# Linear attention in a fused transformer block: each head's kv and output as a product of its own, two heads on halves of TensorE's array

## The reference

```python
h = concatenate([tok(x), txt], axis=1)            # (4, 1024, 256)
y = layernorm(h)
q = elu(split_heads(y @ Wq)) + 1                  # 16 heads, 64 channels
k = elu(split_heads(y @ Wk)) + 1
v = split_heads(y @ Wv)
g = sigmoid(split_heads(y @ Wg + bg))
kv = einsum('bhnd,bhne->bhde', k, v)              # one 64 x 64 matrix a head
k_sum = k.sum(axis=-2)
z = 1.0 / clip(einsum('bhnd,bhd->bhn', q, k_sum), 1e-6)
out = einsum('bhnd,bhde->bhne', q * 64 ** -0.5, kv) * z[..., None] * g
h = h + merge_heads(out) @ Wo
# then two layers of local attention and gated FFN on layernorm(h)
```

## Time and profile before

| | us |
|---|---|
| median of 3 runs (1953.76 to 1954.8) | 1953.86 |
| the profiled execution | 1955.45 |
| its span, from the first to the last instruction | 1953.7 |
| PE busy | 1863.4 (95%) |
| PE weight loads busy | 1624.6 (83%) |
| DVE busy | 1522.5 (78%) |
| ACT busy | 1094.7 (56%) |

### The profile page before, as it was taken

How to read it: one execution, slowest core, us unless ns; L and a number is a source line. 1 busy time by engine, 2 the same in 40 slices (tenths; PEclk the granted TensorE clock), 3 DMA queues, 4 the chain that set the end, 5 groups by cost and what they waited for, 6 DMA issues and landing times. The chain is left out here.

```text
span 1953.7 us, 40490 instructions
## 1 busy us (share of the span) xinstructions
PE 1863.4 (95%) x13340; PEld 1624.6 (83%) x13340; DVE 1522.5 (78%) x4717; ACT 1094.7 (56%) x2551; POOL 431.3 (22%) x319
## 2 busy tenths in 40 slices
PE   8899999999999799999998799979999999989998
PEld 8789889899898578888887688867888888878887
DVE  6888878878687688888887577768888888867777
ACT  4433433433432578888887334427787778853333
POOL 0000000000000335444543000013544454411010
PEclk9999999999999899999999899989999999999999
DMA  9100000000010100000000200010000000000002
GB/s 342 43 1 1 1 1 1 1 1 1 11 57 1 50 7 5 5 5 5 5 4 11 85 12 11 11 44 4 6 4 5 5 5 4 5 22 12 11 11 91
DMA packets 44980, 44.46 MB, mean 23 GB/s; under 512 B 8359, under 2 KB 39387, under 8 KB 44894
## 3 DMA queue, kind: packets, MB, share of 16 engines
q1 hardware_dynamic: 44894, 43.33, 6.7%
HBM read 34.93 MB, written 8.39 MB: 22 GB/s over the span
## 5 line engine op out<-in xcount | busy, mean ns | idle before, releaser
L1117 ACT ACTIVATE l_probs<-l_probs,l_negmax 128x256 f32<-128x256 f32 x512 | 253.2, 496 | 64.8 <-DVE l_negmax L1224 64.8
L1075 POOL TENSOR_TENSOR l_t<-l_t,l_rnorm 128x512 f32<-128x512 f32 x128 | 131.0, 1044 | 301.7 <-DVE l_rnorm L1241 301.7
L117 PE MATMUL ps<-local_w_hi,l_xT 128*128 128x512 f32 x384 | 167.5, 436 | 25.2 <-DVE l_xT L1184 16.1
L1070 POOL TENSOR_TENSOR l_t<-l_t,l_t 128x1024 f32<-128x1024 f32 x64 | 152.6, 2384 | 146.0 <-DVE l_t L1270 146.0
L1123 ACT ACTIVATE l_probsT<-ps 128x512 f32<-128x512 f32 x256 | 138.4, 594 | 40.3 <-PE ps L1375 40.2
L118 PE MATMUL ps<-local_w_lo,l_xT 128*128 128x512 f32 x384 | 155.5, 405 | 0.0
L119 PE MATMUL ps<-local_w_hi,l_xT 128*128 128x512 f32 x384 | 154.5, 402 | 0.0
L117 PE MATMUL ps<-m_hnT_hi,ffn_w_hi 128*128 128x512 f32 (+1 forms) x352 | 143.5, 408 | 10.4 <-DVE m_u L1642 6.1
L486 ACT ACTIVATE attn_exp<-ps 128x512 f32<-128x512 f32 x128 | 76.5, 600 | 133.1 <-PE ps L119 133.1
L1375 PE MATMUL ps<-ident,l_probs 128*128 128x128 f32 x1024 | 135.2, 276 | 6.2 <-ACT l_probsT L1123 6.2
L118 PE MATMUL ps<-m_hnT_lo,ffn_w_hi 128*128 128x512 f32 (+1 forms) x352 | 140.3, 399 | 0.0
(11 more groups left out here) (252 smaller groups left out, 5823.5 us busy)
## 6 DMA issues: line engine op xcount, KB each, us to landing
tok_x<-x SPq DMA_DIRECT2D x16, 512.0 KB, 8.2
m_shifted<-shifted SPq DMA_DIRECT2D x20, 256.0 KB, 2.7
shifted<-x SPq DMA_DIRECT2D x64, 64.0 KB, 1.5
out<-x SPq DMA_DIRECT2D x8, 512.0 KB, 4.5
ffn_w_raw<-ffn_w SPq DMA_DIRECT2D x6, 640.0 KB
local_w_raw<-ffn_wqkv SPq DMA_DIRECT2D x4, 768.0 KB, 5.0
tok_base<-attn_base SPq DMA_DIRECT2D x4, 512.0 KB, 8.7
h<-txt SPq DMA_DIRECT2D x4, 512.0 KB, 8.4
```

What stands on the lines that cost most here:

```text
L117: nc.tensor.matmul(out, wh, mh, start=start, stop=False, skip_group_check=True)
L1070: nc.gpsimd.tensor_tensor(t1[:], t1[:], t2[:], ALU.add).then_inc(s.summed.sem, 1)
L1075: nc.gpsimd.tensor_tensor(v, v, rn[:, a * LH:(a + 1) * LH].unsqueeze(2).to_broadcast([P, LH, DH]), ALU.mult).then_inc(s.rotated.sem, 1)
L1117: last = nc.scalar.activation(v, v, ACT.Exp, bias=nb[:, h:h + 1], scale=-1.0, accum_out=rsum[:, h:h + 1])
```

## The change

`kv_products` and `outputs` make one product for each head in place of one for each pair. In `kv_products` a head's 64 columns of G are the weights and its 65 columns of `attn_wv` the moving side; the two heads of a pair write partitions 0 to 63 and 64 to 127 of the same columns, and so use the two halves of the array's columns. In `outputs` a head's 64 partitions of `attn_qT` and `attn_kv` are used, in the two halves of the array's rows; the even heads write bank 4 and the odd heads bank 5. `attn_kv` then has 65 columns a pair and no zeros, and `take_kv` is two copies. A tile has two groups of 4 pairs, and each of them uses both banks: the next group waits until `gated` has emptied them, for which `attn_o` is counted twice a group. `kv_products` waits for the pieces of G in two steps. Wv is loaded into rows of 64 elements in place of 128.

```diff
-    VC = P + 1
-    OC = P + 2
-    GROUPS = ((0, 3), (3, 6), (6, 8))
-    KV_BANKS = (4, 5, 3)
+    OC = DH + 1
+    PG = PAIRS // 2
...
             def gated(b, n, *groups):
                 for g in groups:
-                    m0, m1 = GROUPS[g]
-                    w = m1 - m0
-                    dve.wait_ge(*s.attn_o_full.after(OB * b + 3 * n + g + 1))
-                    out = ps[:, 4 + (3 * n + g) % 2, 0:w * OC].rearrange("p (m c) -> p m c", c=OC)
...
+                    done = OB * b + 4 * n + 2 * g
+                    dve.wait_ge(*s.attn_o_full.after(FB * b + 2 * n + g + 1))
+                    out = ps[:, 4:6, 0:PG * OC].rearrange("p e (m c) -> p m e c", c=OC)
...
+                    chain(nc.vector.tensor_scalar(heads(zd[:]), out[:, :, :, DH:OC], 1e-6, 2.0 * DH ** 0.5, ALU.max, ALU.mult))
+                    chain(nc.vector.reciprocal(z[:], zd[:]))
+                    nc.vector.tensor_tensor(o1[:, g].rearrange("p (m e d) -> p m e d", e=2, d=DH), out[:, :, :, 0:DH],
+                                            heads(z[:]).to_broadcast([P, PG, 2, DH]), ALU.mult).then_inc(s.attn_o.sem, 1)
+                    dve.wait_ge(*s.attn_o.after(done + 1))
                     if g == 0:
                         dve.wait_ge(*s.attn_b_done.after(GB * b + 2 * n + 2))
...
+                    nc.vector.scalar_tensor_tensor(og[:, n % 2, cols], th[:, n % 2, cols], 1.0, o1[:, g],
+                                                   ALU.add, ALU.mult).then_inc(s.attn_o.sem, 1)
...
             def take_kv(b):
 
                 dve.wait_ge(*s.attn_kv_mm.after(b + 1))
-                dve.wait_ge(*s.attn_set.after(1))
-                for g, (m0, m1) in enumerate(GROUPS):
-                    acc = ps[:, KV_BANKS[g], 0:(m1 - m0) * VC].rearrange("p (m c) -> p m c", c=VC)
-                    for e in range(2):
-                        r = slice(e * DH, (e + 1) * DH)
-                        nc.vector.tensor_copy(kv[r, m0:m1, e * DH:(e + 1) * DH], acc[r, :, e * DH:(e + 1) * DH])
-                        done = nc.vector.tensor_copy(kv[r, m0:m1, P + e:P + e + 1], acc[r, :, P:VC])
+                for g in range(2):
+                    done = nc.vector.tensor_copy(kv[:, g * PG:(g + 1) * PG, :],
+                                                 ps[:, 4 + g, 0:PG * OC].rearrange("p (m c) -> p m c", c=OC))
...
             def kv_products(b):
-                pe.wait_ge(*s.attn_gt.after(4 * b + 4))
-                for g, (m0, m1) in enumerate(GROUPS):
-                    for m in range(m0, m1):
+                for g in range(2):
+                    pe.wait_ge(*s.attn_gt.after(4 * b + 2 * g + 2))
+                    for m in range(g * PG, (g + 1) * PG):
                         for c in range(KC):
-                            last = nc.tensor.matmul(ps[:, KV_BANKS[g], (m - m0) * VC:(m - m0 + 1) * VC],
-                                                    gt[:, c, m * P:(m + 1) * P], wv[:, c, m, :],
-                                                    start=(c == 0), stop=(c == KC - 1))
+                            for e in range(2):
+                                h = 2 * m + e
+                                last = nc.tensor.matmul(ps[e * DH:(e + 1) * DH, 4 + g, m % PG * OC:(m % PG + 1) * OC],
+                                                        gt[:, c, h * DH:(h + 1) * DH], wv[:, c, h, :],
+                                                        start=(c == 0), stop=(c == KC - 1))
...
-            def outputs(b, u, which, *groups):
+            def outputs(b, u, which, g):
...
-                    pe.wait_ge(*s.attn_o.room(OB * b + 3 * n + g, 2))
-                    for m in range(m0, m1):
-                        last = nc.tensor.matmul(ps[:, 4 + (3 * n + g) % 2, (m - m0) * OC:(m - m0 + 1) * OC],
-                                                qt[:, m, which * P:(which + 1) * P], kv[:, m, :],
-                                                start=True, stop=True)
-                    last.then_inc(s.attn_o_full.sem, 1)
+                pe.wait_ge(*s.attn_o.after(OB * b + 4 * n + 2 * g - 1))
+                for m in range(g * PG, (g + 1) * PG):
+                    for e in range(2):
+                        r = slice(e * DH, (e + 1) * DH)
+                        last = nc.tensor.matmul(ps[:, 4 + e, m % PG * OC:(m % PG + 1) * OC],
+                                                qt[r, m, which * P:(which + 1) * P], kv[r, m, :], start=True, stop=True)
+                last.then_inc(s.attn_o_full.sem, 1)
...
-                    outputs(b, u, 0, 0, 1)
+                    outputs(b, u, 0, 0)
                     gates(b, 2 * u + 1, (0,))
-                    outputs(b, u, 0, 2)
+                    outputs(b, u, 0, 1)
                     gates(b, 2 * u + 1, (1,))
                     outputs(b, u, 1, 0)
                     out_products(b, last, u, 1)
-                    outputs(b, u, 1, 1)
...
-                    outputs(b, u, 1, 2)
+                    outputs(b, u, 1, 1)
```

More of the change, by code:

```diff
@@ L238, in _ @@
         def _(pool):
-            nc.gpsimd.memset(K.attn_wv[:, 0, :, P:P + 1], 0.0)
+            nc.gpsimd.memset(K.attn_wv[:, 0, :, DH:DH + 1], 0.0)
         @block.scalar
@@ L419, in attention_phase @@
     (kraw,), _ = mem.place(mem.wb, mem.wa, ("attn_k", [P, 2, INNER], F32))
-    (kv, o1), _ = mem.place(K.attn_rest, mem.norm, ("attn_kv", [P, PAIRS, OC], F32), ("attn_o1", [P, 2, 384], F32))
+    (kv, o1), _ = mem.place(K.attn_rest, mem.norm, ("attn_kv", [P, PAIRS, OC], F32), ("attn_o1", [P, 2, HALF], F32))
     (qt, ex, oth, otl, z, zd), _ = mem.place(
@@ L494, in tanh_ @@
             def tanh_(b, n, halves=(0, 1)):
-                act.wait_ge(*s.attn_o.after(OB * b + 3 * (n - 1)))
+                act.wait_ge(*s.attn_o.after(OB * b + 4 * (n - 1)))
                 for half in halves:
@@ L635, in gated @@
                 for g in groups:
-                    m0, m1 = GROUPS[g]
-                    w = m1 - m0
-                    dve.wait_ge(*s.attn_o_full.after(OB * b + 3 * n + g + 1))
-                    out = ps[:, 4 + (3 * n + g) % 2, 0:w * OC].rearrange("p (m c) -> p m c", c=OC)
-                    chain(nc.vector.tensor_scalar(zd[:, 0:2 * w].rearrange("p (m e) -> p m e", e=2), out[:, :, P:OC],
-                                                  1e-6, 2.0 * DH ** 0.5, ALU.max, ALU.mult))
-                    chain(nc.vector.reciprocal(z[:, 0:2 * w], zd[:, 0:2 * w]))
@@ L647, in gated @@
+                    dve.wait_ge(*s.attn_o.after(done + 1))
                     if g == 0:
                         dve.wait_ge(*s.attn_b_done.after(GB * b + 2 * n + 2))
-                    nc.vector.scalar_tensor_tensor(og[:, n % 2, m0 * P:m1 * P], th[:, n % 2, m0 * P:m1 * P], 1.0,
-                                                   o1[:, g % 2, 0:w * P], ALU.add, ALU.mult).then_inc(s.attn_o.sem, 1)
+                    cols = slice(g * HALF, (g + 1) * HALF)
+                    nc.vector.scalar_tensor_tensor(og[:, n % 2, cols], th[:, n % 2, cols], 1.0, o1[:, g],
+                                                   ALU.add, ALU.mult).then_inc(s.attn_o.sem, 1)
@@ L713, in batch @@
                     norm.deviation(nc, chain)
-                gated(b, 0, 0, 1, 2)
+                gated(b, 0, 0, 1)
                 gated(b, 1, 0)
@@ L722, in batch @@
                     ot_lo(b, last, u, 0)
-                    gated(b, 2 * u - 1, 2)
+                    if u > 1:
+                        gated(b, 2 * u - 1, 1)
                     query_feature(b, u, 2)
@@ L843, in outputs @@
                 pe.wait_ge(*s.attn_kv.after(b + 1))
-                for g in groups:
-                    m0, m1 = GROUPS[g]
-                    pe.wait_ge(*s.attn_o.room(OB * b + 3 * n + g, 2))
-                    for m in range(m0, m1):
-                        last = nc.tensor.matmul(ps[:, 4 + (3 * n + g) % 2, (m - m0) * OC:(m - m0 + 1) * OC],
-                                                qt[:, m, which * P:(which + 1) * P], kv[:, m, :],
-                                                start=True, stop=True)
-                    last.then_inc(s.attn_o_full.sem, 1)
+                pe.wait_ge(*s.attn_o.after(OB * b + 4 * n + 2 * g - 1))
[5 more added lines that the diff above has]
+                last.then_inc(s.attn_o_full.sem, 1)
             def out_transposes(b, last, u, which):
@@ L855, in out_transposes @@
                 n = 2 * (u - 1) + which
-                pe.wait_ge(*s.attn_o.after(OB * b + 3 * n + 3))
+                pe.wait_ge(*s.attn_o.after(OB * b + 4 * n + 4))
                 for half in range(2):
@@ L903, in batch @@
                 gates(b, 0)
-                outputs(b, 0, 0, 0, 1)
+                outputs(b, 0, 0, 0)
                 gates(b, 1, (0,))
-                outputs(b, 0, 0, 2)
+                outputs(b, 0, 0, 1)
                 gates(b, 1, (1,))
@@ L910, in batch @@
                 outputs(b, 0, 1, 1)
-                outputs(b, 0, 1, 2)
                 for u in range(1, STAGES):
@@ L1958, in build @@
```

(6 more changed lines are left out.)

23 lines of the change are left out of this document (10 added, 13 removed).

## The result

The changed kernel takes 1976.5 us (median of 4 runs, 1975.03 to 1977.68) against 1954.33 (4 runs, 1953.76 to 1957.2): 1.0112 times as long, 95% interval 1.0098 to 1.0125, or about 22 us more. Forecast were 13.0 more and 1966.9, range 1955 to 1977. The profiled execution's span grew from 1953.7 to 1973.5. The first matmul of the first local attention moved from 635.5 to 657.0, so the attention and what lies ahead of it lost 21.6 us, and the later phases, which the change doesn't touch, gave 1.8 back.

The account below looks back on a forecast made before the run. PE's instruction stream was taken to bound the linear attention. Terms +20.8 (`outputs`), -8.8 (`kv_products`), +0.3 (tail) and +0.7 (Wv's load) gave +13.0 us on the median of 1953.86: 1966.9 us, range 1955 to 1977.

Parts of the forecast that it names:

- `outputs`, forecast +20.8: 64 groups of half-array products in the linear attention at 1.22 us each, 78.1 us against 57.3.
- The load at 0.107 for 128 columns: In `outputs`, loading 128 weight columns takes about 0.107 us, so a pair goes at 0.110, not 0.055.
- the switch of 0.20 on either side: Going between full-array and half-array work costs PE 0.20 us before and after each `outputs` group.
- Rival A: In `outputs` the weight load does not bind: -3.5 in place of +20.8, 1942.6 us in all; 10%.
- Rival B: The mode switch around `outputs` costs only 0.10 a side: 12.8 us less, 1954, no change; 7%.
- `kv_products`, forecast -8.8: 64-column weights, 2.17 us without a wait: 2.4 us gained in each of three batches, 1.6 in the first.
- Single buffer, forecast 0 with 0.2 us to spare: `outputs` groups now need both banks, but VectorE empties them before PE's next group: no wait, cost 0.
- Rival C: The single buffer binds, VectorE late by 0.2 to 0.5 us at 32 places: +6 to +16 us, 1973 to 1983; 15%.
- Wv's load, forecast +0.7: Wv in pieces of 256 bytes for 512 slows the token phase: nothing to 3.6 us, taken as +0.7.
- The tail, forecast +0.3: At the attention's end, the last `outputs` group's longer VectorE work lies open before the last transposes: +0.3 us.

Follow-up runs that it names:

- run 6: Changed kernel with 64 of a tile's 128 tokens as weights in `outputs`, half of the outputs left out; 1949.46 us.
- run 7: Changed kernel with `outputs` moving 33 of the 65 columns, half of each head's output left out; 1974.46 us.
- run 8: Changed kernel with each `outputs` group's four even heads first, then the four odd ones; 2008.93 us.
- run 1: Changed kernel with the last `outputs` group of a stage put back ahead of the transposes; 1969.5 us, ratio 1.0073 to the kernel before.
- run 3: Changed kernel with Wv loaded in rows of 4096 bytes into Wo's place and spread by the subtraction; 1971.6 us, ratio 1.0088 to the kernel before.
- run 2: Kernel before with the new `kv_products` and Wv layout, `outputs` by pairs of heads, eight copies in `take_kv`; 1956.37 us, ratio 1.0011.
- run 4: Changed kernel with 64 unused bytes a partition ahead of Wo; 1977.82 us.
- run 5: Kernel before with 64 unused bytes a partition ahead of Wo, nothing else changed; 1958.1 us.
- run 10: Changed kernel with the group ahead of the transposes again, Wv in 4096-byte rows, Wo 8192 bytes below its old address; 1962.0 us, ratio 1.0047 to the kernel before.
- run 11: Kernel before with Wv loaded in rows of 4096 bytes in place of 512, nothing else; 1953.9 us, ratio 1.0001.
- run 9: Kernel before with new `kv_products`, four-copy `take_kv` on two engines, 4096-byte Wv rows, Wo moved, its low part later in first batch; 1942.23 us, ratio 0.9942.

## Why the prediction was right, and where its sum was short

The direction and the mechanism were right; the size came out 9 us short, nearly all of it in terms that the sum has at zero or doesn't have. The median lies in the forecast range by 0.5 us, and two of the four executions lie above it: that the range held owes something to luck.

**`outputs`, forecast +20.8.** 64 groups at 1.24 us are 79.4 for 57.3: +22.0. The load at 0.107 for 128 columns, the switch of 0.20 on either side (0.19 and 0.20 here) and the streaming of 0.055 were each as the rows of the local attention said; runs 6 and 7 show that the weights' columns bind, and run 8 that one half alone goes at the same 0.112. Rivals A and B are out. The Trainium skill, "TensorEngine Tiling (Array Packing)", section "Theoretical Speedup", gives up to twice the rate for such a shape. No part of that came here: 16 records at half the array took 1.05 us, where 8 records of the whole array take 0.90. In `kv_products`, with 64 columns of weights, it nearly did: a pair of records takes 0.058 us where one record took 0.112.

**`kv_products`, forecast -8.8.** 2.07 us and 0.14 ahead of it for 2.17 forecast, and no wait: a gain of 2.35 a batch. In the first batch VectorE was late as said: PE's work lay 2.67 us later than before at the `queries` ahead of `kv_products` and 0.93 later at `gates`, a gain of 1.7 for 1.6. Together -8.8.

**Single buffer, forecast 0 with 0.2 us to spare.** No wait on `attn_o` in the trace: VectorE's product L641 ends at 440.98 where PE's next group starts at 441.42. Rival C is out, though it gave nearly the time that was measured, by another mechanism.

**The step that failed: the moved group.** The front part says that the group between `out_products` and the transposes is gone, and the prediction never asked what it covered. It covered `residual`, which reads the bank that the transposes fill. Price: 0.58 us in nine places, 5.2 us; putting it back gave 7 (run 1).

**Wv's load, forecast +0.7.** The attention started 1.3 us later, and rows of 4096 bytes bring 3.3 (run 3), so the load was all of it; run 6, whose clock is full up to there, starts as late as the changed kernel. The sum had 0.7 by judgement between 0 and 3.6.

**The clock, not in the sum.** The half clock behind the attention's start cost 1.7 more in the profiled execution. A fall of this kind between 62 and 71 us is in the profiles of the changed kernel and runs 2, 3, 4, 5, 7, 8, 10 and 11 and is absent before and in runs 1, 6 and 9, of which run 1 has one at 126 us. Neither the load's pieces nor the time of the start sorts them, so it is told and not explained, and it may be the execution's and not the kernel's.

**What the prediction did not price:** the shift of Wo by 64 bytes. In the kernel before a stage's two `out_products` take 2.73 and 2.82 us, a few times 2.82 and 2.82, here 2.88 and 2.87; over the attention that is 2.5 us, and run 5 has the same.

**Short waits of before that are gone, not in the sum.** Ahead of the first `outputs` of a batch PE waited 0.29 us in three batches and 0.65 in the last, in the changed kernel no longer: -1.5. The busy time of the earlier trace rows, which is of a stretch inside a batch, can't show them.

**The tail, forecast +0.3.** The last wait grew from 2.43 to about 3.0 us, some +0.6. But part of what lies behind it runs at the clock's lower level in both kernels, and in the changed one the clock came back sooner. First the kernel before, then the changed one:

```profile
624.00:628.00 4.00, 3.46 (x17) 3.09 (x16) 2.04 (x4) 0.74 (x2) 0.00 (x0) 0.50 0.00 0
628.00:632.00 4.00, 4.00 (x27) 4.00 (x27) 0.42 (x1) 0.00 (x0) 0.00 (x0) 0.71 0.00 0
```

```profile
644.00:648.00 4.00, 2.37 (x10) 2.03 (x11) 2.54 (x5) 1.19 (x2) 0.00 (x0) 0.50 0.00 0
648.00:652.00 4.00, 4.00 (x26) 4.00 (x26) 0.93 (x3) 0.00 (x0) 0.00 (x0) 0.67 0.00 0
```

Before, 23 records of the last `out_products` go at 0.21 us in place of 0.12, in the changed kernel 12. From the last record of `outputs` to the local attention are 15.1 us before and 15.0 after: -0.1.

Together: 22.0 - 8.8 + 5.2 + 1.3 + 1.7 + 2.5 - 1.5 - 0.1 = 22.3, against 21.6 measured at the local attention's start. 0.7 us are left: 0.3 of the later start are gone again before the first `kv_products`, and the rest is within the rounding of 64 groups.

## What to carry to other kernels

Splitting a product over halves of the array pays when the weights get narrower, not when the moving side does: count loads, columns of weights and switches before counting columns moved. `kv_products` had 64 weight columns and went from 3.6 to 2.2 us with its switches, `outputs` kept 128 and lost. When a piece of work leaves its place in a hand-written order, ask what it hid there, from the banks that its neighbours share; and see whether a tile whose size changes shifts others.

## What the runs showed of the hardware

- A matmul over half the array's rows with 128 columns of weights goes at 0.112 us a pair whether 65 or 33 columns move; with 64 columns of weights at 0.06 (runs 6 and 7, `kv_products`). A switch of the mode costs 0.19 us ahead of a group with 128 weight columns and 0.14 with 64, and 0.20 behind it. The Trainium skill, same page, "Key Properties", says that a switch drains the engine; here is its price.
- In one half alone, records with 128 weight columns follow each other every 0.112 us (run 8), as a pair of both halves does. There the second half began when five of the first half's eight records had begun, ahead of the other three: alternating the halves gives 1.05 us for 16 records, one after the other 1.54.
- 64 bytes in the address of a moving fp32r operand change 24 records of 256 columns from 2.73 to 2.88 us (run 5), 128 bytes to 2.83 (run 4), and 8192 bytes leave 2.73 (run 10).
- The granted clock can fall to its lower level for some 3.4 us where PE starts after a wait, which costs 1.7 us. In run 11's profile it took back most of what an earlier start had won; in run 9's it did not fall.
